# Hybrid conv-attention kernel: the next image's front part at other slots, and query tiles coupled in another order

## The reference

```
x = x + proj(softmax(l2norm(q) @ l2norm(k)^T * temp) @ v)   # over channels: 8 heads of 24, 1x1 convolutions
t = tokens(x)                                               # 1024 tokens of 192
t = t + attention(layer_norm(t))                            # 6 heads of 32, causal, scale 1/sqrt(192)
t = t + ffn(layer_norm(t))                                  # 192 -> 768 -> 192, sign weights, gelu
x = image(t)                                                # the ffn quantizes by the maximum over a group of 6 images
```

## Time and profile before

| | us |
|---|---|
| median of 3 runs | 4501.67 |
| lowest, highest | 4501.24, 4506.31 |
| profiled execution | 4509.63 |
| its span, first to last instruction | 4507.8 |
| PE busy | 4014.6 |
| DVE busy | 3041.2 |
| ACT busy | 2974.6 |

### The profile page before, as it was taken

How to read it: one execution, slowest core, us unless ns; L and a number is a source line. 1 busy time by engine, 2 the same in 40 slices (tenths; PEclk the granted TensorE clock), 3 DMA queues, 4 the chain that set the end, 5 groups by cost and what they waited for, 6 DMA issues and landing times.

```text
span 4507.8 us, 114786 instructions
## 1 busy us (share of the span) xinstructions
PE 4014.6 (89%) x39240; PEld 2916.3 (65%) x39240; DVE 3041.2 (67%) x5559; ACT 2974.6 (66%) x6669; POOL 364.2 (8%) x375
## 2 busy tenths in 40 slices
PE   6999999879999898999989879999898999999887
PEld 4767665666777646767665667777646777664665
DVE  5666666766666677666666766666676666666765
ACT  3676666657777655676666657776655666666666
POOL 1000002000000110000002000000110000002000
PEclk7999999989999999999999989999999999999999
DMA  2111111011221101111111011221101111111011
GB/s 72 37 37 37 44 37 29 0 51 37 51 50 37 37 0 43 37 37 37 44 37 29 1 51 37 53 48 37 37 0 43 37 37 41 40 37 29 0 43 43
DMA packets 48832, 161.01 MB, mean 36 GB/s; under 512 B 12612, under 2 KB 13126, under 8 KB 48198
## 3 DMA queue, kind: packets, MB, share of 16 engines
q1 hardware_dynamic: 48326, 154.40, 14.2%
HBM read 28.52 MB, written 25.17 MB: 12 GB/s over the span
## 4 chain that ended last, share of the span: by engine, by line
PE 65%; DVE 13%; issue 12%; ACT 6%; POOL 1%; DMA 1%; DVEq 1%; ACTq 1%; SPq 0%; POOLq 0%
PE PT L698 11%; PE OUT L718 10%; PE S L684 6%; DVE nmax L1231 5%; PE PT L824 5%; PE S L743 5%; PE S L794 3%; PE S L642 3%; PE FR L642 3%; PE FR L586 2%; ACT work L952 2%; DVE work L385 2%; DVE XT L1100 2%; PE FR L649 1%; PE S L649 1%
## 5 line engine op out<-in xcount | busy, mean ns | idle before, releaser
L1231 DVE TENSOR_REDUCE nmax<-S 128x1 f32<-128x256 f32 (+7 forms) x1536 | 1146.1, 753 | 940.4 <-PE S L686 930.3
L952 ACT ACTIVATE work<-S,nmax 128x256 f32<-128x256 f32 (+7 forms) x1536 | 1138.8, 742 | 611.8 <-DVE nmax L1231 592.3
L698 PE MATMUL PT<-ident,work 128*128 128x128 f32 x6912 | 1079.3, 280 | 92.9 <-DVE work L385 57.0
L698 PEld LDWEIGHTS PT<-ident,work 128*128 128x128 f32 x6912 | 750.7, 143 | 260.0 <-ACT work L952 54.4
L385 DVE COPY work<-PT 128x512 f32<-128x512 f32 x768 | 524.0, 682 | 45.3 <-PE PT L698 38.0
L944 ACT ACTIVATE work<-PT 128x256 f32<-128x256 f32 (+3 forms) x768 | 338.7, 441 | 155.3 <-PE PT L698 148.3
L684 PE MATMUL S<-KS,QS 128*128 128x512 f16 (+3 forms) x1152 | 325.5, 337 | 109.2 <-ACT work L952 75.6
L684 PE MATMUL S<-odd 128*128 128x512 f16 (+3 forms) x1152 | 316.2, 329 | 71.7 <-ACT work L952 68.0
L686 PE MATMUL S<-causal,identb 128*128 128x128 bf16 x1536 | 339.5, 221 | 0.0
L956 ACT ACTIVATE work<-PT 128x512 f32<-128x512 f32 (+3 forms) x768 | 332.9, 433 | 1.5 <-PE PT L698 1.4
L743 PE MATMUL S<-odd,W1b 128*128 (+1 forms) x1080 | 262.1, 395 | 49.9 <-ACT work L995 41.5
(11 more groups left out here) (209 smaller groups left out, 6010.4 us busy)
## 6 DMA issues: line engine op xcount, KB each, us to landing
X<-in_x SPq DMA_DIRECT2D x32, 768.0 KB, 5.3
odd<-hi_z SPq DMA_DIRECT2D x128, 192.0 KB, 4.2
odd<-odd SPq DMA_DIRECT2D x128, 192.0 KB, 4.3
out_y<-work SPq DMA_DIRECT2D x64, 384.0 KB, 3.7
QS<-hi_z SPq DMA_DIRECT2D x64, 192.0 KB, 3.8
QS<-odd SPq DMA_DIRECT2D x64, 192.0 KB, 4.0
KS<-hi_z SPq DMA_DIRECT2D x64, 192.0 KB, 4.5
KS<-odd SPq DMA_DIRECT2D x64, 192.0 KB, 4.7
```

The source lines that it names most:

```text
L698: last = tr(bank[:, P * (j - c0):P * (j - c0) + P], PS[m % 2][:, m // 2 % 2, P * j:P * j + P], ident[:, :])
L952: A(PS[n % 2][:, n // 2 % 2, 0:w], S[:, n % 2, 0:w], ACT.Exp, bias=nmax[:, n % MAXES:n % MAXES + 1], accum_out=rowsum[:, sum_col(n):sum_co ...
L1231: v.tensor_reduce(nmax[:, n % MAXES:n % MAXES + 1], S[:, n % 2, 0:P * (qtile(n) + 1)], AX.X, ALU.max, negate=True).then_inc(max_made, 1)
```

## The change

`TILES` becomes (2, 4), (0, 6), (1, 5), (3, 7): widths 3 and 5, 1 and 7, 2 and 6, 4 and 8. `SLOTS` becomes two tables. `FIRST` is used for the front part made beside a group's first image; it begins at slot 0. The new `SLOTS` is used for the others; it begins at slot -2, that is, two slots before the end of the image before, whose own front part is then finished. The three engines look the table up by the image's place.

```diff
-TILES = [(1, 7), (3, 5), (0, 6), (2, 4)]
+TILES = [(2, 4), (0, 6), (1, 5), (3, 7)]

-SLOTS = {"xt0": 0, "xt1": 1, "xt2": 2, "xt3": 4, "g0a": 5, "g0": 6, "g1a": 7, "g1": 8, "wg0": 9, "wg1": 10,
-         "na": 11, "rb": 15, "u": 18, "mt": 19, "t0": 20, "t1": 21, "t2": 22, "t3": 23, "z0": 31, "z1": 32,
-         "z2": 33, "z3": 34, "qk0": 35, "qk1": 36, "qk2": 37, "qk3": 38, "qk4": 39, "qk5": 40, "v0": 41, "v1": 42,
-         "v2": 43, "v3": 44}
-SMALL_SLOTS = {"norms": 12, "rdiag": 13, "logits": 16, "xexp": 17, "attn": 17.5, "ln_stats0": 22, "ln_stats1": 25,
-               "ln_norm0": 27, "ln_norm1": 28, "ln_round0": 28.5, "ln_round1": 29}
+FIRST = {"xt0": 0, "xt1": 0, "xt2": 1, "xt3": 3, "g0a": 4, "g0": 6, "g1a": 7, "g1": 7, "wg0": 8, "wg1": 9,
+         "na": 10, "rb": 14, "u": 18, "mt": 19, "t0": 20, "t1": 21, "t2": 22, "t3": 23, "z0": 31, "z1": 32,
+         "z2": 33, "z3": 34, "qk0": 34, "qk1": 36, "qk2": 37, "qk3": 38, "qk4": 39, "qk5": 40, "v0": 42, "v1": 43,
+         "v2": 44, "v3": 45}
+FIRST_SMALL = {"norms": 11, "rdiag": 12, "logits": 15, "xexp": 16, "attn": 16.5, "ln_stats0": 22, "ln_stats1": 25,
+               "ln_norm0": 27, "ln_norm1": 28, "ln_round0": 29, "ln_round1": 30}
+
+SLOTS = {"xt0": -2, "xt1": -2, "xt2": -1, "xt3": 0, "g0a": 1, "g0": 3, "g1a": 4, "g1": 4, "wg0": 6, "wg1": 8,
+         "na": 9, "rb": 13, "u": 17, "mt": 18, "t0": 19, "t1": 20, "t2": 21, "t3": 22, "z0": 30, "z1": 31,
+         "z2": 31, "z3": 32, "qk0": 33, "qk1": 34, "qk2": 36, "qk3": 37, "qk4": 39, "qk5": 40, "v0": 42, "v1": 43,
+         "v2": 44, "v3": 45}
+SMALL_SLOTS = {"norms": 10, "rdiag": 11, "logits": 14, "xexp": 15, "attn": 15.5, "ln_stats0": 21, "ln_stats1": 24,
+               "ln_norm0": 26, "ln_norm1": 27, "ln_round0": 28, "ln_round1": 29}
+
+def slots_of(u):
+    return SLOTS if u else FIRST
...
         def fronts_at(slot, run, parts, fronts):
             for u in range(fronts):
-                for name, at in parts:
+                for name, at in parts(u):
                     if UNITS * u + int(at) == slot:
                         run(name, u)
```

More of the change, by code:

```diff
@@ L149, with small_slots_of @@
 assert FRONT_STEPS % 2 == 0
-SLOTS = {"xt0": 0, "xt1": 1, "xt2": 2, "xt3": 4, "g0a": 5, "g0": 6, "g1a": 7, "g1": 8, "wg0": 9, "wg1": 10,
-         "na": 11, "rb": 15, "u": 18, "mt": 19, "t0": 20, "t1": 21, "t2": 22, "t3": 23, "z0": 31, "z1": 32,
-         "z2": 33, "z3": 34, "qk0": 35, "qk1": 36, "qk2": 37, "qk3": 38, "qk4": 39, "qk5": 40, "v0": 41, "v1": 42,
-         "v2": 43, "v3": 44}
-SMALL_SLOTS = {"norms": 12, "rdiag": 13, "logits": 16, "xexp": 17, "attn": 17.5, "ln_stats0": 22, "ln_stats1": 25,
-               "ln_norm0": 27, "ln_norm1": 28, "ln_round0": 28.5, "ln_round1": 29}
+FIRST = {"xt0": 0, "xt1": 0, "xt2": 1, "xt3": 3, "g0a": 4, "g0": 6, "g1a": 7, "g1": 7, "wg0": 8, "wg1": 9,
[12 more added lines that the diff above has]
+    return SLOTS if u else FIRST
+def small_slots_of(u):
+    return SMALL_SLOTS if u else FIRST_SMALL
 def hybrid_kernel(nc, x, wa, wb, wv, wpt, bp, temp, w3, w1, b1, w2, b2, out):
@@ L729, in attention @@
                             last.then_inc(pt_full[i % 2], 1)
-                    fronts_at(n, lambda name, u: front_part(name, g, u + 1), SLOTS.items(), fronts)
+                    fronts_at(n, lambda name, u: front_part(name, g, u + 1), lambda u: slots_of(u).items(), fronts)
                     if images == GS and EARLY.get(n, "").startswith("turn"):
@@ L912, in front_part, with order_of @@
                 o.then_inc(front_free[bank_of(name)], 1)
-            order = list(SLOTS.items()) + [("xexp", SMALL_SLOTS["xexp"])]
-            order.sort(key=lambda a: a[1])
-            for name, _ in order:
+            def order_of(u):
+                return sorted(list(slots_of(u).items()) + [("xexp", small_slots_of(u)["xexp"])], key=lambda a: a[1])
+            for name, _ in order_of(0):
                 front_part(name, 0, 0)
@@ L956, in attention @@
                             pt_copy(act, lambda o, x: A(o, x, ACT.Copy), g, images, i)
-                    fronts_at(n, lambda name, u: front_part(name, g, u + 1), order, fronts)
+                    fronts_at(n, lambda name, u: front_part(name, g, u + 1), order_of, fronts)
                     if images == GS and EARLY.get(n, "").startswith("norm"):
@@ L1168, in front_part, with order_of @@
                     dve.sem_inc(free, 1)
-            order = list(SLOTS.items()) + [a for a in SMALL_SLOTS.items() if a[0] != "xexp"]
-            order.sort(key=lambda a: a[1])
-            for name, _ in order:
+            def order_of(u, behind=0):
+                small = [a for a in small_slots_of(u).items() if a[0] != "xexp"]
+                all_at = [(name, at + behind * name.startswith("qk")) for name, at in list(slots_of(u).items()) + small]
+                return sorted(all_at, key=lambda a: a[1])
+            for name, _ in order_of(0):
                 if name == "mt":
@@ L1190, in _ @@
             dve.sem_inc(w12_ready, 1)
-            later = sorted([(name, at + name.startswith("qk")) for name, at in order], key=lambda a: a[1])
             def stats2(b, tiles):
@@ L1239, in attention @@
                             add_to_t1(g, i, c[2])
-                    fronts_at(n, lambda name, u: front_part(name, g, u + 1), later, fronts)
+                    fronts_at(n, lambda name, u: front_part(name, g, u + 1), lambda u: order_of(u, 1), fronts)
                     if images == GS and n in EARLY:
```

## The result

The changed kernel takes 4584.67 us (median of 4 runs, 4580.45 to 4592.51) against 4502.23; the ratio is 1.0183, 95% interval 1.0168 to 1.0197. It is slower by 82 us, where 63 us less were forecast. The profiled execution took 4586.6 with a span of 4584.8.

A forecast was written before the change was run, and what follows sets the result against it. PE was taken as the bound only where fed, with 14.7 us of waits an image. Gains of 62 (25 x 2.5) + 6 - 5 = 63 us gave 4446.6 profiled, forecast median 4439; own range 4405 to 4472, wider range 4388 to 4502.

The forecast's parts named there:

- The prices of PE's work: Start-to-start prices of scores, transposes, triples and front parts: 88.1 us of work an image, leaving 14.7 of 102.8 as waits.
- the walk of slots 10 to 18: Small softmax, queues followed with durations from the rows: 3.3 us of PE waits an image in place of 4.2.
- the clock: Rival, 4470 us: clock falls in new slots 12 to 16 of each image, 25 x 1.25 = 31 us given back; chance 0.12.
- the sum: Waits of an image added over three stretches: 3.3 + 4.9 + 3.9 = 12.1 us against 14.7, a gain of 2.5.
- `mt`'s wait: In the small softmax, U's copy queued behind slot 17's exponential, late by DVE's wait for `xexp`: 0.7 us.
- Slots 19 to 33: Layer-norm statistics and norms placed beside other units: 4.9 us of waits an image in place of 7.0.
- The rest: Remaining slots of an image: 3.4 us of waits kept, plus 0.5 for `na` in slot 9, which needs `wg1`'s copy.
- the other thin stretch: Argument against the clock rival: of the two stretches with waits, the one outside new slots 12 to 16 is filled.
- Waits only move: Rival, 4500 us: DVE's and ACT's steps are not fewer, so small waits eat the 2.5 us an image; chance 0.12.
- Handovers behind wide exponentials: Slower rival, 4560 us: five parts one slot behind their needed copy cost 1.0 us more each, 62 in all; chance 0.10.
- First images: Six images with `FIRST`, `u` staying at 18 and `qk0` behind `z3`: 1 us gained each, 6 in all.
- more than forecast: Rival, 4385 us: handovers cost nothing, 5.6 x 25 is 140 less the ends, half way taken, 115; chance 0.12.

The follow-up runs named there:

- after: The changed kernel, with both the new tile order and the new slot tables, against the kernel before: 4584.67 us against 4502.23, ratio 1.0183.
- the fillers: 28 idle matmuls of 512 columns an image added on PE ahead of waits in slots 8, 9, 17 and 29 of the changed kernel: 4490.05 us.
- the second kernel that adds fillers to it: Changed kernel with `attn` at 16.5, plus 16 idle matmuls an image in slots 8 to 11 and 29 where their bank is free: 4452.94 us.

## Why the prediction was wrong

- **The prices of PE's work** held. In slots without a wait the measured time is the priced one: slot 22 of after took 2.46 for 2.46, slot 34 2.18 for 2.18.
- **Two steps failed**: the walk of slots 10 to 18, and the clock, to which the sum gave nothing. Measured and forecast are 145 us apart. Over 25 images some 98 us of that (3.9 each) come with the clock, and 48 (1.9 each) are waits at full clock; this is an estimate that prices the images in sixth place like the others.
- **Slots 10 to 18**. The walk gave 3.3 us of waits, the measurement is 8.1 (20.4 for 12.3). With the fillers, at full clock, it is 5.1. One wait, 1.85, is as large as what the walk lacked there: the sentence that `attn` is done 0.9 before PE has finished slot 17's triple let PE reach the triple without regard to DVE, whose copy of slot 16 is queued behind `attn`. The transposes of slot 17 need it. The walk had found the wait ahead of them (1.6, measured 1.71) and DVE's wait for `xexp` (measured 1.77), but did not ask what else was behind it. The other 3.0 come with the clock.
- **`mt`'s wait** of 0.7 was forecast and is not there; that the wait ahead of it gave ACT the time is likely, but no run shows it.
- **Slots 19 to 33**: 4.9 forecast, 5.6 at full clock, 6.4 as measured (mean of 20 images). The new place of `qk0` costs the 1.0 that was forecast; slots 28 and 29 have 3.0 together where the walk had 2.8.
- **The rest**: 3.9 forecast, 3.5 measured; but its parts were not those. `wg1` and `na` in slots 8 and 9 wait 1.8 where 0.5 was forecast for `na`, and the other waits are shorter than before.
- **At full clock**, then, an image takes 102.2 in place of 102.8: the gain is 0.6, not 2.5.
- **The clock** was the right rival with the wrong size and chance (0.12). I priced one fall of 1.25 an image. There are two to four, counting a stretch of 6.8 us as two; one of 3.4 costs 1.3 to 1.6, and after has 3.9 an image in all. The five images in sixth place were in the 25 and lost more than the others, 4.5 each against 3.2. The argument against the rival, that the other thin stretch is filled, missed that the edit itself lengthens PE's waits in the first one, and that a thin order of tiles was put around them. The fillers, which do nothing but keep PE active, bring the clock of the 20 images from between 0.94 and 0.97 back to 1.00; the rule of the Trainium skill ("TensorE: Matmul & The Clock Gate", What's actually happening) that activity releases the throttle pointed the right way.
- **Waits only move** is what the full-clock part turned out to be. **Handovers behind wide exponentials**, the slower rival, had the sign right and the cause wrong: `g0a` waits 0.4, `qk0` 1.0, `z3` 0.2, `mt` nothing, `wg1` and `na` together 1.8, and with all of them an image at full clock is still 0.6 below before.
- **First images** gained 8.4 for the six (forecast 6), and that is luck: the new tiles alone gave 29.8, and `FIRST`, which was to help, took 21.4 back. The ends of attention and the rest lost 2.6 (forecast 5).
- **One sum** of the rivals does not come out: half of the way from 63 us to the 140 of "more than forecast" is about 102 us, not 115.

What stays open is what exactly decides a fall. The tables alone have the same two waits in slot 17 and kept the clock in 16 of 20 images; after, with 1.4 us less work around them, did not. With `attn` at 16.5 the wait of 1.70 alone, with the new tiles, brought no fall in slot 17 in 20 images, and one in 20 in the second kernel that adds fillers to it. No run here separates the length of the waits from the work around them.

## What to carry to other kernels

When a step moves on an in-order engine, list everything that is queued behind the place where it waits, copies that free a buffer above all, and follow who waits for each; moving `attn` by one slot was worth 111 us. Where the tensor engine stands for a microsecond or two, look at what stands around the wait and behind it: a fall of the clock costs as much as the wait itself, and idle matmuls in the wait show in one run how much of a loss is the clock's. Two edits that do little harm alone, one making waits and one thinning the work around them, have to be measured together. An edit made of several parts should be measured by part: `FIRST` lost 21 us behind a gain of the tiles.

## What the runs showed of the hardware that was not expected

- Adding 28 matmuls of 512 columns an image (6.0 us of PE's time) made the kernel 95 us faster, with the waits of slot 17 as long as before (2.42 us against 2.41).
- The falls fall into a rhythm: the images of after repeat 105.2 and 106.5 in turn, with clocks of 0.97 and 0.95 (in three of the five groups the first of them took 108.1), though every image runs the same program. Images of the kernel with `attn` at 16.5 took 100.2, 101.5 or 103.0 by the number of falls alone.
- A triple of seven blocks takes 1.66 us at 2.4 GHz and 3.13 in after's slot 17; the four matmuls of `u` behind it 0.88 in place of 0.73.
